# Two-head attention on one core: reciprocal three steps later, scaling one step later, SyncE's small transfers split and reordered

## The chip, the cores and the metric

One core of one Trainium2 chip runs the whole program. The metric is device microseconds of one execution. The kernel before took 3663.01 us (median of three; 3644.68 to 3670.26).

## The reference, cut to what matters

The program is a graph layer followed by a transformer block on x of shape (2, 2048, 512). Only the block's attention is touched by the change:

```
qkv = (h @ Wqkv + bqkv).reshape(B, L, 3, H, HD)        # B=2, L=2048, H=16, HD=32
attn = softmax(einsum('blhd,bmhd->bhlm', q, k) * HD ** -0.5, axis=-1)
out = einsum('bhlm,bmhd->blhd', attn, v).reshape(B, L, D)
return out @ Wproj + bproj
```

The softmax's division is done last: unnormalized exponentials are multiplied with the values, and the product is scaled by the reciprocal of the exponentials' sum.

## The kernel before, in words

The phases run one after the other: setup, graph layer, q/k/v projections, attention, output projection, MLP. Attention is `attention_phase`, and it is one straight program for each of the five engines; semaphores tie them together. Nothing schedules it at run time: the order on each engine is the order of the code.

The work is cut into 16 pairs g (two heads of one batch element). A pair has 32 steps. Steps 0 to 15 are its first half, steps 16 to 31 its second; a half is half of the query rows (1024 of 2048, for both heads), and a step is one tile of 128 keys against those rows, in four chunks c of 512 rows. Halves are numbered n = 0 to 31.

- **TensorE** (PE) makes per chunk one score matmul (`att_pS`, L1333) and one matmul for the row maxima of the next pair (`att_pM`, L1286). Score banks rotate over three, maxima banks over four, so TensorE waits for ScalarE or VectorE when one of them falls behind. At chunk 2 of each even step it also makes the value products of two earlier steps (`att_pO`, L1301). At step 4 of a half, chunk 2, it sums up the exponentials of the previous half (`finish`, L1315): 16 matmuls with a tile of ones (L1307).
- **ScalarE** (ACT) takes the exponential of each score chunk (L1218). At step 0, chunk 2, it copies the finished products of the half before to `oc` (L1190, function `copy`); before that it waits until the stores of the half before that one have left `oc` (`o_stored`, L1189). At step 4, chunk 2, it copies the sums to `rec` (L1198). It also issues the loads of a later pair (`LOADS`: steps 3, 6, 9, 12, 15, 18 and the values at step 2): six of these seven lie in a pair's first half.
- **VectorE** (DVE) reduces each maxima chunk (L1233). After the four chunks of step `INVERT` of a half it makes the reciprocal of the packed sums (L1252, function `invert`); it waits there for four small transfers (`z_packed`).
- **GpSimd** (POOL) adds up nine of a half's sixteen probability tiles with eight additions (L1155), sends four others to DMA additions (L1135), and, after addition number `SCALED`, scales the output of the half before: `oc` times `rec` (L1125, function `scale`), for which it waits for `z_spread`.
- **SyncE** (SP) issues the small transfers, in one order. For each half: the first two 1 MB copies of the DMA sums (`send_first`, L1077), then `reciprocals`: pack the sums of four rows into 128 partitions (L1084, four transfers), wait for the reciprocal, keep it in DRAM (L1086), wait for that to land, spread it over the partitions (L1089, four transfers). After that `store` (L1062) waits for the scaling and issues the four output stores (L1068). In a pair's second half SyncE also sends the turned maxima of the next pair (`rows`, L1055) between `reciprocals` and `store`.

The chain of a half's output is therefore: sums copied (L1198), packed, inverted on VectorE, kept, spread, scaled on GpSimd, stored, and then ScalarE may overwrite `oc` at step 0 of the next half.

Of the kernel before, what the change touches and what calls it, by code (L numbers as in the profile page):

```python
# [78 lines left out]
def raw(ap):  # L79

    return ap.bitcast(F32)
# [844 lines left out]
def attention_phase(nc, io, keep):  # L926

    with ExitStack() as ctx:
        m = Mem(nc, ctx, "att")
        NG = B * H // 2  # L930
# [13 lines left out]
        NA = len(ADDED) - 1  # L944
        FINISH = 4
        LOADS = [3, 6, 9, 12, 15, 18]
        INVERT = 6
        SCALED = 5
        ident = keep["ident"]

        qs = [m.sb(f"qs{i}", [KD + 2, 2, S], F32R) for i in range(U)]
# [30 lines left out]
        def m_tile(g, step, c):  # L982

            ahead = 1 if step < ST - LEAD else 2
            return (g + ahead, (step + LEAD) % ST * 4 + c) if g + ahead < NG else None
# [35 lines left out]
        def exps(g, step):  # L1021
            return turns_of[g, step, 3] + 1

        def turn(g):
            return place[f"turned {g}"]
# [8 lines left out]
        def load_part(eng, g, i):  # L1034
            k, at = g % U, slice(g % 2 * S, (g % 2 + 1) * S)
            if i < 3:
                dst, src = qs[k][i * HD:(i + 1) * HD], q_v[(0, 0, 1)[i], g // 2, :, :, at]
            else:
                dst, src = ks[k][(i - 3) * HD:(i - 2) * HD], k_v[(0, 1, 0)[i - 3], g // 2, :, :, at]
            eng.dma_start(raw(dst), src).then_inc(loaded[k], 16)  # L1040

        def load_values(eng, g):
            hp = g // 2
            eng.dma_start(V[g % 2][:], v_v[:, g % 2, :, hp * 2 * HD:(hp + 1) * 2 * HD]).then_inc(v_loaded[g % 2], 16)

        @block.sync
        def _(sp):
            def load(g):
                for i in range(6):
                    load_part(sp, g, i)  # L1050

            def load_v(g):
                load_values(sp, g)

            def rows(g):  # L1055

                sp.wait_ge(m_read, turn(g) + 1)
                for h in range(2):
                    sp.dma_start(raw(qs[g % U][KD + h:KD + h + 1]).rearrange("a h (t n) -> a (h t) n", n=P),
                                 raw(nm[:, h, :])).then_inc(top_rows[g % U], 16)  # L1060

            def store(n):  # L1062

                g, half = divmod(n, 2)
                sp.wait_ge(o_ready, n + 1)
                for c in range(4):
                    dst = o_v[g // 2, c // 2, :, g % 2, (2 * half + c % 2) * 512:(2 * half + c % 2 + 1) * 512]
                    sp.dma_start(dst, oc[c * HD:(c + 1) * HD]).then_inc(o_stored, 16)  # L1068

            def send_first(n):  # L1070

                if n >= 1:
                    sp.wait_ge(s_done, turns_of[n - 1] + 1)
                for i in range(2):
                    step = n % 2 * MT + CHAINS[i][0]
                    sp.wait_ge(exp_done, exps(n // 2, step))
                    sp.dma_start(gathered[i][:], prob[step % PR][:]).then_inc(first_sent[i], 16)  # L1077

            def reciprocals(n):

                sp.wait_ge(exp_done, turns_of[n] + 1)
                for c in range(4):
                    row = rec[c * HD:c * HD + 1, :].rearrange("a (i x) -> a i x", x=16)
                    sp.dma_start(packed[c * HD:(c + 1) * HD, :], row).then_inc(z_packed, 16)  # L1084
                sp.wait_ge(inverted, n + 1)
                sp.dma_start(io["z_d"][n % 2].rearrange("c (i x) -> (c i) x", x=16), packed[:]).then_inc(z_kept, 16)  # L1086
                sp.wait_ge(z_kept, 16 * (n + 1))
                for c in range(4):
                    sp.dma_start(rec[c * HD:(c + 1) * HD, :], io["z_d"][n % 2, c:c + 1, :].to_broadcast([HD, 512])).then_inc(z_spread, 16)  # L1089

            load(0)
            load(1)
            load_v(0)
            load_v(1)
            load(2)
            rows(0)
            for g in range(NG):
                if g >= 1:
                    send_first(2 * g)
                    reciprocals(2 * g - 1)  # L1100
                    store(2 * g - 1)
                else:
                    send_first(0)
                send_first(2 * g + 1)
                reciprocals(2 * g)
                if g + 1 < NG:
                    rows(g + 1)
                store(2 * g)
            reciprocals(2 * NG - 1)
            store(2 * NG - 1)  # L1110
            sp.wait_ge(o_stored, 64 * 2 * NG)

        @block.gpsimd
        def _(pool):
# [12 lines left out]
            def send(n, i, j):  # L1127

                step = n % 2 * MT + CHAINS[i][j]
                pool.wait_ge(exp_done, exps(n // 2, step))  # L1130
                if j == 1:
                    pool.wait_ge(first_sent[i], (n + 1) * 16)
                else:
                    pool.wait_ge(sent[i], (n * 2 + 1) * 16)
                nc.gpsimd.dma_start(gathered[i][:], prob[step % PR][:], accum_op=ALU.add).then_inc(sent[i], 16)  # L1135

            for g in range(NG):
                for half in range(2):
                    n = g * 2 + half
                    for i in range(1, NA + 1):  # L1140
                        step = half * MT + ADDED[i]
                        pool.wait_ge(exp_done, exps(g, step))
                        new = prob[step % PR]
                        if i == SCALED + 1 and n >= 1:
                            pool.wait_ge(o_ready, n)
# [10 lines left out]
                        if ADDED[i] in SENT_BEHIND:  # L1156
                            send(n, *SENT_BEHIND[ADDED[i]])
                        if i == SCALED and n >= 1:
                            pool.wait_ge(added, n * NA + i)
# [67 lines left out]
        def _(dve):  # L1227
            def maxima(g, q):
                if q == 0 and g >= 1:
                    dve.wait_ge(top_ready, g)  # L1230
                at = place[g, q]
                dve.wait_ge(m_done, at + 1)
                nc.vector.tensor_reduce(mx[:, q // 4, q % 4:q % 4 + 1], bank(at)[:], AX.X, ALU.max).then_inc(m_read, 1)  # L1233
# [15 lines left out]
            def invert(n):  # L1249

                dve.wait_ge(z_packed, 64 * (n + 1))
                nc.vector.reciprocal(packed[:], packed[:]).then_inc(inverted, 1)  # L1252
# [10 lines left out]
            for g in range(NG):  # L1263
                for step in range(ST):
# [5 lines left out]
                    for c in range(4):  # L1270
                        if m_tile(g, step, c):
                            maxima(*m_tile(g, step, c))
                    if step % MT == INVERT and n >= 0:
                        invert(n)
# [492 lines left out]
def build(nc, io, upto=9):  # L1767

    for name, shape, dt in [("x1_d", (B * S, D), F32), ("gate_d", (2, B * S // 512, P, D), F32),
                            ("qk_d", (2, 2, D, B * S), F32), ("v_d", (B * S, D), F32),  # L1770
                            ("o_d", (D, B * S), F32), ("z_d", (2, 4, 512), F32), ("x2_d", (B * S, D), F32), ("h2_d", (D, B * S), F32)]:
        io[name] = nc.dram_tensor(name, shape, dt, kind="Internal").ap()
    with ExitStack() as ctx:
        m = Mem(nc, ctx, "keep")
        keep = {"cols": m.sb("cols", [P, NCOLS]), "ident": m.sb("ident", [P, P]),
                "modA": m.sb("modA", [P, 2, B * S // 512 * DC]), "modB": m.sb("modB", [P, 2, B * S // 512 * DC])}
        with ExitStack() as early:
            e = Mem(nc, early, "graph")
            keep["floor4"] = e.sb("floor4", [4, 1])
            keep["wl_bc"] = e.sb("wl_bc", [P, 2 * NONGT * L])  # L1780
            keep["bb"] = e.sb("bb", [P, 1])
            keep["LW"] = e.sb("LW", [P, 2, B, DC, D + 2 * HM], F32R)
            keep["VB"] = e.sb("VB", [GM, B, 2, DC, P])
            keep["r4"] = e.sb("r4", [4, B, D + 2 * HM], F32R)
            setup_phase(nc, io, keep)
            graph_phase(nc, io, keep)
        if upto > 1:
            qkv_phase(nc, io, keep)
        if upto > 2:
            attention_phase(nc, io, keep)  # L1790
        if upto > 3:
            proj_phase(nc, io, keep)
        if upto > 4:
            mlp_phase(nc, io, keep)
# [45 lines left out]
```

## Time and profile before

| | |
|---|---|
| profiled execution | 3662.34 us |
| its span, first to last instruction | 3660.6 us |
| mean granted TensorE clock | 0.939 of full |
| TensorE matmul busy | 3351.8 us (92%) |
| VectorE busy | 2061.6 us (56%) |
| ScalarE busy | 1520.4 us (42%) |
| GpSimd busy | 1617.7 us (44%) |
| VectorE idle before the maxima reductions (L1233) | 366.1 us, for TensorE |
| TensorE idle before the maxima matmuls (L1286) | 115.6 us, 94.2 of it for VectorE |
| TensorE idle before the score matmuls (L1333) | 8.2 us, 7.9 of it for ScalarE |
| TensorE, 980 to 2650 us (attention without its end) | 1569.96 us busy of 1670.00, clock 0.96 |

The span is what lies between the first and the last instruction on the core; 1.7 us of the execution's time lie around it. A row of the timeline merges neighbouring instructions of one kind: its start, the time it covers, the count, and in brackets how long the engine stood idle before it and what ended that. Matmuls overlap, so the sum of their durations is more than the time they take. The clock is a share of 2.4 GHz, 0.5 being 1.2 GHz.

### The profile page before, as it was taken

How to read it: one execution, taken by the hardware profiler on the slowest of the kernel's cores; microseconds unless marked ns; L12 is line 12 of the kernel's file. 1: busy time of each engine (PE TensorE's matmuls, PEld its weight loads, DVE VectorE, ACT ScalarE, POOL GpSimd, SP SyncE). 2: the span in 40 equal slices, each digit the busy share in tenths (PEclk: the TensorE clock that was granted, in tenths of full speed). 3: DMA queues.
4: the chain of work that ended last, by engine and by line, in shares of the span. 5: the costliest groups of instructions: out<-in, count | busy, mean ns of one | idle time of the engine just before them, and what ended most of it. 6: DMA issues, size and time to landing. Idle time of an engine off the chain costs nothing. (4 is left out here: it accounts for less than half of the span.)

```text
span 3660.6 us, 45573 instructions
## 1 busy us (share of the span) xinstructions
PE 3351.8 (92%) x17004; PEld 2242.4 (61%) x17004; DVE 2061.6 (56%) x3419; ACT 1520.4 (42%) x2751; POOL 1617.7 (44%) x621
## 2 busy tenths in 40 slices
PE   7989996997999999999999999999995679999999
PEld 6478884775554544555545545445434568888887
DVE  1278884443976766767767767777506922221222
ACT  0011113432066655656656656566661242222222
POOL 1033331001087777777778767778884400000000
PEclk9899997998599999999999999999997889999999
DMA  4222324445256676676766666766564641111110
GB/s 151 81 83 89 98 79 158 171 155 174 64 133 161 145 167 149 147 167 149 169 156 159 155 163 149 169 153 150 128 150 165 231 153 46 41 41 37 37 32 24
DMA packets 202646, 460.45 MB, mean 126 GB/s; under 512 B 62811, under 2 KB 84571, under 8 KB 171742
## 3 DMA queue, kind: packets, MB, share of 16 engines
q1 hardware_dynamic: 144286, 267.16, 21.8%
q0 software_dynamic: 18432, 134.23, 18.5%
q10 hardware_dynamic: 39744, 56.63, 6.2%
q8 instruction: 113, 1.85, 0.2%
q14 instruction: 71, 0.58, 0.1%
HBM read 167.28 MB, written 88.34 MB: 70 GB/s over the span
## 5 line engine op out<-in xcount | busy, mean ns | idle before, releaser
L1233 DVE TENSOR_REDUCE att_mx<-att_pM 128x1 f32<-128x512 f32 x2048 | 1250.8, 681 | 366.1 <-PE att_pM L1286 365.4
L1218 ACT ACTIVATE att_prob<-att_pS 128x512 f32<-128x512 f32 x2048 | 1047.3, 618 | 576.6 <-PE att_pS L1333 574.6
L1155 POOL TENSOR_TENSOR att_acc<-att_acc,att_prob 128x2048 f32<-128x2048 f32 x224 | 1026.6, 4583 | 337.8 <-ACT att_prob L1218 323.7
L1286 PE MATMUL att_pM<-att_ks,att_qs 96*128 96x512 f32 x2048 | 863.2, 436 | 115.6 <-DVE att_mx L1233 94.2
L1333 PE MATMUL att_pS<-att_qs,att_ks 98*128 98x512 f32 x2048 | 855.0, 421 | 8.2 <-ACT att_prob L1218 7.9
L1333 PEld LDWEIGHTS att_pS<-att_qs,att_ks 98*128 98x128 f32 x2048 | 390.3, 191 | 358.0 <-issue 204.7
L1286 PEld LDWEIGHTS att_pM<-att_ks,att_qs 96*128 96x128 f32 x2048 | 412.0, 201 | 245.4 <-DVE att_mx L1233 167.7
L1301 PE MATMUL att_pO<-att_prob,att_V 128*32 128x512 f32 x4096 | 513.6, 621 | 0.0
L1696 DVE TENSOR_TENSOR mlp_us<-mlp_tu,mlp_us 128x512 fp32r<-128x512 f32 x128 | 89.6, 700 | 537.5 <-ACT mlp_us L1669 537.5
L1739 PE MATMUL mlp_pu<-mlp_hs,mlp_W 128*128 128x512 f32 x1536 | 371.3, 391 | 20.2 <-DVE mlp_W L1688 20.2
L1758 PE MATMUL mlp_pa<-mlp_W,mlp_us 128*128 128x512 f32 x1536 | 368.8, 389 | 0.0
L1739 PEld LDWEIGHTS mlp_pu<-mlp_hs,mlp_W 128*128 128x128 f32 x1536 | 290.0, 189 | 81.1 <-issue 20.6
L1758 PEld LDWEIGHTS mlp_pa<-mlp_W,mlp_us 128*128 128x128 f32 x1536 | 288.3, 188 | 59.8
L1681 POOL TENSOR_TENSOR mlp_hs<-mlp_hf,mlp_hs 128x512 fp32r<-128x512 f32 x32 | 41.3, 1291 | 600.5 <-ACT mlp_hs L1647 600.5
L1668 ACT ACTIVATE mlp_tu<-mlp_pu,keep_cols 128x512 f32<-128x512 f32 x128 | 88.3, 690 | 505.6 <-PE mlp_pu L1739 505.6
L1301 PEld LDWEIGHTS att_pO<-att_prob,att_V 128*32 128x32 f32 x4096 | 109.8, 112 | 259.9 <-ACT att_prob L1218 161.6
L1155 POOL TENSOR_TENSOR att_acc<-att_prob 128x2048 f32<-128x2048 f32 x32 | 146.8, 4589 | 190.2 <-ACT att_prob L1218 190.2
L921 PE MATMUL qkv_pq<-qkv_hs,qkv_W 128*128 128x512 f32 x768 | 188.8, 402 | 2.4 <-DVE qkv_hs L861 2.4
L921 PEld LDWEIGHTS qkv_pq<-qkv_hs,qkv_W 128*128 128x128 f32 x768 | 146.0, 193 | 32.9 <-issue 2.8
L1530 PE MATMUL prj_pp<-prj_W,prj_os 128*128 128x512 f32 x384 | 98.0, 419 | 47.6 <-POOL prj_os L1479 47.4
L1252 DVE RECIPROCAL att_packed<-att_packed 128x16 f32<-128x16 f32 x32 | 8.1, 253 | 230.3 <-DMA att_packed<-att_rec 230.3
L1115 POOL MEMSET att_ones<- 128x32 f32 x1 | 0.1, 125 | 306.8 <-POOLq L107 306.8
(183 smaller groups left out, 3042.5 us busy)
## 6 DMA issues: line engine op xcount, KB each, us to landing
att_gathered<-att_prob POOLq DMA_DIRECT2D x128, 1024.0 KB, 8.2
att_gathered<-att_prob SPq DMA_DIRECT2D x64, 1024.0 KB, 5.0
qk_d<-qkv_qs SPq DMA_DIRECT2D x64, 512.0 KB, 2.7
att_qs<-qk_d ACTq DMA_DIRECT2D x39, 512.0 KB, 4.7
att_ks<-qk_d ACTq DMA_DIRECT2D x39, 512.0 KB, 6.1
gat_xT<-in_xT SPq DMA_DIRECT2D x32, 256.0 KB, 3.2
gat_xrow<-in_x SPq DMA_DIRECT2D x32, 256.0 KB, 2.8
x_d<-gat_x SPq DMA_DIRECT2D x32, 256.0 KB, 2.1
```

What stands on the lines that cost most here:

```text
L921: last = nc.tensor.matmul(out[:], a, r, start=n + c == 0, stop=n == 2 and c == DC - 1)
L1155: nc.gpsimd.tensor_tensor(acc[half][:], old[:], new[:], ALU.add).then_inc(added, 1)
L1218: nc.scalar.activation(prob[step % PR][:, c, :], pS[at % 3][:], ACT.Exp, scale=SCALE).then_inc(exp_done, 1)
L1233: nc.vector.tensor_reduce(mx[:, q // 4, q % 4:q % 4 + 1], bank(at)[:], AX.X, ALU.max).then_inc(m_read, 1)
L1286: nc.tensor.matmul(bank(at)[:], qs[k][0:KD, h, t * P:(t + 1) * P], ks[k][0:KD, h, mc * 512:(mc + 1) * 512], start=True, stop=True).then_in ...
L1301: last = nc.tensor.matmul(pO[c * HD:(c + 1) * HD, :], V[g % 2][:, mt, (c // 2) * HD:(c // 2 + 1) * HD], prob[step % PR][:, c, :], start=mt ...
L1333: nc.tensor.matmul(pS[at % 3][:], ks[k][:, h, mt * P:(mt + 1) * P], qs[k][:, h, lc * 512:(lc + 1) * 512], start=True, stop=True).then_inc( ...
L1530: last = nc.tensor.matmul(pp[nt][:], os_[s][:, k, c, nt * P:(nt + 1) * P], W[:, w, c, :], start=n + c == 0, stop=n == 2 and c == DC - 1)
L1668: nc.scalar.activation(tu[j % 2][:], pu[j % 4][:], ACT.Gelu, bias=bias)
L1696: nc.vector.tensor_tensor(us[j % 2][:, 1, :], tu[j % 2][:], us[j % 2][:, 0, :], ALU.subtract).then_inc(u_lo, 1)
L1739: last = nc.tensor.matmul(pu[j % 4][:], W1[:, k, c, j * P:(j + 1) * P], hs[s][:, w, c, :], start=q + c == 0, stop=q == 2 and c == DC - 1)
L1758: last = nc.tensor.matmul(pa[nt][:], us[j % 2][:, k, nt * P:(nt + 1) * P], W2[:, w, j, :], start=j + q == 0, stop=j == MC - 1 and q == 2)
```

## The change

`INVERT` goes from 6 to 9: VectorE makes the reciprocal after the maxima of step 9 of a half. `SCALED` goes from 5 to 6: GpSimd scales after its sixth addition. `reciprocals` is cut in three functions, called one after the other everywhere but in a pair's second half, where the turned maxima now go out between the kept reciprocal and its spreading. No instruction is added or removed.

```diff
-        INVERT = 6
-        SCALED = 5
+        INVERT = 9
+        SCALED = 6
...
-            def reciprocals(n):
+            def pack(n):
...
+            def keep_inverted(n):
+
                 sp.wait_ge(inverted, n + 1)
                 sp.dma_start(io["z_d"][n % 2].rearrange("c (i x) -> (c i) x", x=16), packed[:]).then_inc(z_kept, 16)
+
+            def spread(n):
+
                 sp.wait_ge(z_kept, 16 * (n + 1))
...
                 send_first(2 * g + 1)
-                reciprocals(2 * g)
+                pack(2 * g)
+                keep_inverted(2 * g)
                 if g + 1 < NG:
                     rows(g + 1)
+                spread(2 * g)
                 store(2 * g)
```

The rows below are the order of instructions on an engine, with tile names and counts; line numbers of the kernel after are 12 higher from the split on (L1252 is L1264 there, L1125 is L1137).

VectorE before, one pair from a reciprocal in its second half to the next pair's (`att_mx` are the maxima, `att_top` and `att_nm` their final forms, `att_packed` the sums):

```order
L1252 RECIPROCAL att_packed<-att_packed 128x16
L1233 TENSOR_REDUCE att_mx<-att_pM 128x1 x12
L1237 TENSOR_REDUCE att_top<-att_mx 128x32
L1233 TENSOR_REDUCE att_mx<-att_pM 128x1 x4
L1245 CAST att_nm<-att_pM 32x128
L1247 TENSOR_TENSOR att_nm<-att_pM,att_nm 32x128
L1233 TENSOR_REDUCE att_mx<-att_pM 128x1 x48
```

VectorE in the changed kernel, the same place:

```order
L1264 RECIPROCAL att_packed<-att_packed 128x16
L1249 TENSOR_REDUCE att_top<-att_mx 128x32
L1245 TENSOR_REDUCE att_mx<-att_pM 128x1 x4
L1257 CAST att_nm<-att_pM 32x128
L1259 TENSOR_TENSOR att_nm<-att_pM,att_nm 32x128
L1245 TENSOR_REDUCE att_mx<-att_pM 128x1 x60
```

The reciprocal stands twelve reductions later, directly ahead of the pair's final maxima.

GpSimd before, from a half's fourth addition on (`att_oc` is the output being scaled):

```order
L1155 TENSOR_TENSOR att_acc<-att_acc,att_prob 128x2048
L1135 DMA att_gathered<-att_prob 128x2048
L1155 TENSOR_TENSOR att_acc<-att_acc,att_prob 128x2048
L1135 DMA att_gathered<-att_prob 128x2048
L1125 TENSOR_TENSOR att_oc<-att_oc,att_rec 128x512
L1155 TENSOR_TENSOR att_acc<-att_acc,att_prob 128x2048 x3
```

GpSimd in the changed kernel, the same place:

```order
L1167 TENSOR_TENSOR att_acc<-att_acc,att_prob 128x2048
L1147 DMA att_gathered<-att_prob 128x2048
L1167 TENSOR_TENSOR att_acc<-att_acc,att_prob 128x2048
L1147 DMA att_gathered<-att_prob 128x2048
L1167 TENSOR_TENSOR att_acc<-att_acc,att_prob 128x2048
L1137 TENSOR_TENSOR att_oc<-att_oc,att_rec 128x512
L1167 TENSOR_TENSOR att_acc<-att_acc,att_prob 128x2048 x2
```

The scaling stands behind one more addition, that of step 12.

SyncE before, in a pair's second half (`z_d` is the kept reciprocal, `att_nm` the turned maxima, `o_d` the output in DRAM):

```order
L1084 DMA att_packed<-att_rec 32x1x16 x4
L1086 DMA z_d<-att_packed 128x16
L1089 DMA att_rec<-z_d 32x512 x4
L1059 DMA att_qs<-att_nm 1x32x128 x2
L1068 DMA o_d<-att_oc 32x512 x4
```

SyncE in the changed kernel, the same place:

```order
L1084 DMA att_packed<-att_rec 32x1x16 x4
L1089 DMA z_d<-att_packed 128x16
L1059 DMA att_qs<-att_nm 1x32x128 x2
L1095 DMA att_rec<-z_d 32x512 x4
L1068 DMA o_d<-att_oc 32x512 x4
```

The spreading stands behind the two transfers of the turned maxima; in a pair's first half SyncE's order is as before.

## Rows read from the trace of the kernel before

**Rows 1.** Waits, 900 to 2650 us: who, for whom: us, times, longest.

```profile
DVE att_packed L1252 <- DMA att_packed<-att_rec: 109.9, 29, 7.4
PE att_pM L1286 <- DVE att_mx L1233: 94.2, 27, 6.8
...
ACT att_oc L1190 <- DMA o_d<-att_oc: 13.0, 5, 3.3
```

**Rows 2.** ScalarE timeline: start, busy us, work, count, idle before, releaser.

```profile
1059.43 0.60 ACT L1198 ACTIVATE att_rec<-att_pS 128x512 f32<-128x512 f32 x1 [4.75 <-PE att_pS L1307]
...
1382.17 0.60 ACT L1190 ACTIVATE att_oc<-att_pO 128x512 f32<-128x512 f32 x1 [3.25 <-DMA o_d<-att_oc]
...
1734.13 0.60 ACT L1198 ACTIVATE att_rec<-att_pS 128x512 f32<-128x512 f32 x1 [4.75 <-PE att_pS L1307]
...
1770.38 0.60 ACT L1190 ACTIVATE att_oc<-att_pO 128x512 f32<-128x512 f32 x1 [1.29 <-PE att_pO L1301]
...
1785.42 0.60 ACT L1198 ACTIVATE att_rec<-att_pS 128x512 f32<-128x512 f32 x1 [4.80 <-PE att_pS L1307]
...
1842.75 0.60 ACT L1198 ACTIVATE att_rec<-att_pS 128x512 f32<-128x512 f32 x1 [4.75 <-PE att_pS L1307]
...
2610.73 0.60 ACT L1198 ACTIVATE att_rec<-att_pS 128x512 f32<-128x512 f32 x1 [4.75 <-PE att_pS L1307]
```

**Rows 3.** VectorE's timeline, 1776 to 1798.1 us.

```profile
1776.84 4.88 DVE L1233 TENSOR_REDUCE att_mx<-att_pM 128x1 f32<-128x512 f32 x8 [0.94 <-PE att_pM L1286]
1786.06 4.88 DVE L1233 TENSOR_REDUCE att_mx<-att_pM 128x1 f32<-128x512 f32 x8 [4.35 <-PE att_pM L1286]
...
1797.95 0.25 DVE L1252 RECIPROCAL att_packed<-att_packed 128x16 f32<-128x16 f32 x1 [5.38 <-DMA att_packed<-att_rec]
```

**Rows 4.** TensorE's matmuls in its timeline, near 1383, 1799 and 1808 us.

```profile
1383.31 0.50 PE L1333 MATMUL att_pS<-att_qs,att_ks 98*128 98x512 f32 x1 [1.49 <-ACT att_prob L1218]
...
1798.81 0.80 PE L1286 MATMUL att_pM<-att_ks,att_qs 96*128 96x512 f32 x1 [4.86 <-DVE att_mx L1233]
...
1801.24 3.21 PE L1301 MATMUL att_pO<-att_prob,att_V 128*32 128x512 f32 x16
...
1808.32 1.92 PE L1301 MATMUL att_pO<-att_prob,att_V 128*32 128x512 f32 x16
```

**Rows 5.** SyncE timeline of DMA issues: start, us spent issuing, count.

```profile
1754.57 1.97 SPq L1059 DMA_DIRECT2D att_qs<-att_nm  x2
1760.55 4.21 SPq L1068 DMA_DIRECT2D o_d<-att_oc  x4
...
1798.23 0.35 SPq L1086 DMA_DIRECT2D z_d<-att_packed  x1
1805.84 2.87 SPq L1089 DMA_DIRECT2D att_rec<-z_d  x4
1818.14 4.12 SPq L1068 DMA_DIRECT2D o_d<-att_oc  x4
```

**Rows 6.** GpSimd's timeline, 1758 to 1775 us.

```profile
1758.97 1.55 POOL L1125 TENSOR_TENSOR att_oc<-att_oc,att_rec 128x512 f32<-128x512 f32 x1
1760.66 14.07 POOL L1155 TENSOR_TENSOR att_acc<-att_acc,att_prob 128x2048 f32<-128x2048 f32 x3
```

**Rows 7.** Stretches: length, busy us by engine, clock, DMA share, GB/s.

```profile
1766.13:1768.13 2.00, 2.00 (x11) 1.52 (x9) 2.00 (x4) 2.00 (x6) 2.00 (x1) 1.00 0.01 3
...
1810.13:1812.13 2.00, 2.00 (x12) 1.63 (x9) 1.18 (x2) 1.42 (x3) 1.59 (x3) 1.00 0.34 68
...
1826.13:1828.13 2.00, 2.00 (x18) 0.75 (x11) 1.30 (x3) 0.63 (x2) 1.86 (x2) 1.00 0.29 57
```

**Rows 8.** Landings of output stores (L1068), issued near 1760, 1818, 2758 us.

```profile
DMA to landing us min/median/max: 3.6/4.6/5.2
...
DMA to landing us min/median/max: 5.5/6.2/6.8
...
DMA to landing us min/median/max: 1.7/1.7/1.8
```

More of the change, by code:

```diff
@@ L1099, in _ @@
                     send_first(2 * g)
-                    reciprocals(2 * g - 1)
+                    pack(2 * g - 1)
+                    keep_inverted(2 * g - 1)
+                    spread(2 * g - 1)
                     store(2 * g - 1)
@@ L1104, in _ @@
                 send_first(2 * g + 1)
-                reciprocals(2 * g)
+                pack(2 * g)
+                keep_inverted(2 * g)
                 if g + 1 < NG:
                     rows(g + 1)
+                spread(2 * g)
                 store(2 * g)
-            reciprocals(2 * NG - 1)
+            pack(2 * NG - 1)
+            keep_inverted(2 * NG - 1)
+            spread(2 * NG - 1)
             store(2 * NG - 1)
```

## The prediction, made before the changed kernel had run

> **What bounds the kernel now.** I read the list of waits of the attention first, then the timelines of the five engines over two neighbouring halves, and last the DMA share of short stretches. The waits show TensorE as the engine that is almost always at work, and two places where it is made to stand. The reciprocal on VectorE waits 109.9 us in 29 times for the packed sums to land; behind it the maxima reductions are late, the four maxima banks fill, and TensorE stands 94.2 us in 27 times for a reduction [rows 1]. The other place is ScalarE's copy of the output, which waited 13.0 us in 5 times for the output stores before it [rows 1].
>
> Then I took the sums copy (L1198, once per half) as a clock of the loop. From the first to the copy of 2610.73 there are 28 periods, 1551.3 us [rows 2]. They alternate: the one from 1734.13 takes 51.3 us, the next, from 1785.42, takes 57.3 [rows 2]. Added up, the 14 short ones give 729.2 us and the 14 long ones 822.1. The long ones run mostly through a pair's first half, where four of the 0.5 MB loads are issued as well.
>
> What would a period be without a stop? VectorE's groups of eight reductions repeat every 0.94 + 4.88 = 5.82 us, and the group behind the sums comes 9.22 us after the one before it [rows 3]: 7 x 5.82 + 9.22 = 50.0 us. So 28 x 50.0 = 1400 us, and **151 us** are lost to stops: 29 in the short periods, 122 in the long ones.
>
> A stop costs more than its idle time. In the long period VectorE waited 5.38 us [rows 3], TensorE stood 4.86 us, and behind that 16 value matmuls took 3.21 us where they otherwise take 1.92 [rows 4]: TensorE ran at the lower of its two clock levels (1.2 for 2.4 GHz) for a few microseconds. The period is 57.3 - 50.0 = 7.3 us too long, so the slow stretch costs 7.3 - 4.9 = 2.4 us. Of the copy's wait, TensorE feels only a part: 3.25 us of waiting on ScalarE [rows 2] became 1.49 us on TensorE [rows 4], since it has score banks to work on; the cover is 1.76 us. That case too had slow matmuls behind it.
>
> **The change, part by part.** Times are counted from a period's sums copy.
>
> 1. *Reciprocal three steps later.* Three steps are 12 reductions, one and a half groups, 8.7 us. VectorE stood ready at 1797.95 - 5.38 = 1792.57 [rows 3], +7.15. It will be ready at +15.9. The sums landed at 1797.95, +12.5, in this long period; the longest of the 29 waits was 7.4 us [rows 1], which is +14.5. So all 29 waits are covered, with 1.4 us to spare in the worst. A load by ScalarE (step 9) that the stop used to delay now goes out at about +11 and may take a little of that; I keep small leftovers of 0.4 us a period. The reciprocal itself (0.25 us, rows 3) costs the same in either place, and TensorE's banks cover it. Removed: 151 us at most.
>
> 2. *Keeping and spreading.* SyncE now issues the kept reciprocal at about +16.2, where it was +12.8 in the long period [rows 5]. From there to the spreading it was 7.6 us [rows 5], the spreading takes 2.9 us to issue and the landing some 4: +30 to +33. In a short period the turned maxima are ready at 1754.57, +20.4 [rows 5], and their two issues (1.97 us) now stand ahead of the spreading. It goes out at about +21.3 to +22.5 instead of +12.9, and lands before +30. Who waits for it is GpSimd's scaling alone.
>
> 3. *Scaling one addition later.* It began at 1758.97 [rows 6], +24.8, and that period had 1.2 us of stop. An addition is 14.07 / 3 = 4.69 us [rows 6], and that of step 12 starts when that step's exponentials are there, 5.8 us after step 10's. I put the scaling 5.45 us later, at +29.1 without a stop, and its end 1.6 later at +30.7 [rows 6]. In the long period the spreading is not there yet: the scaling begins about +32 and ends at +33.6. GpSimd's two last additions move by the same few microseconds; they are needed only by the next sums, over 12 us later, so I cost that at nothing. The cover is gone if the scaling comes later than about +38.
>
> 4. *The output stores.* This is what is late next. `oc` must be empty when ScalarE reaches its copy: 1770.38, +36.25 [rows 2], less the 1.2 us of stop: +35.05. The four stores took 4.21 us to issue [rows 5] and the last up to 5.2 us to land in the short period, 4.12 [rows 5] and up to 6.8 in the long one; with nothing else under way, at the end of the attention, they landed in 1.7 [rows 8]. The quickest issue of four small transfers took 2.87 us [rows 5]. The bounds for the time from the scaling's end to an empty `oc` are thus 4.6 and 10.9 us. Which end holds is told by the DMA share. In the short period the DMA engines fall to 0.01 at 1766.13, +32.0 [rows 7]: the big transfers are out, and stores issued at about +30.8 land near the lower bound, around +35.4. No wait beyond the 1.76 us of cover. In the long period the DMA engines are at work until 1826.13 to 1828.13, +41 to +42, but with thin stretches behind the stop (0.34 at 1810.13, rows 7); with the stop gone the same work should be through at +38. Stores issued from +33.7 on then land about +39.5: ScalarE waits 4.5 us, TensorE stands 4.5 - 1.76 = 2.7 us, and 2.4 us of slow clock follow, 5.1 in all.
>
> In the last three halves there are no more maxima matmuls behind the reciprocal, so nothing is won there, and a late store may cost up to 5 us in all; I take 2.
>
> **The sum**, against the profiled execution's 3662.3 us (the median of the runs shown is 3663.0): the short periods win 29 and keep 14 x 0.4 = 6; the long ones win 122 and give back 14 x 5.1 = 71; the end costs 2. 3662.3 - 29 + 6 - 122 + 71 + 2 = **3590 us**.
>
> **What a page says of such transfers.** The row first: small transfers took 3.6 to 6.8 us to land while others were under way, and 1.7 when alone [rows 8]. The Trainium skill (DMA: Bandwidth & Descriptors, section Anatomy of one DMA) gives about 2.0 us of fixed cost for a DMA, mostly the receipt of the last write, and next to nothing more for 64 KB; it would put the landing of the small transfers at some 2 us in every period. By that rule the scaling would not wait, no copy would, and the sum would be that of rival A below. The rows of the crowded halves speak against it as a full account, the row at the end agrees with it.
>
> **The rivals.**
>
> *A. Everything is covered.* The DMA engines, with the stops gone, are through early enough that the stores of the long periods land within 35.05 + 1.76 = +36.8. That needs an end of the scaling by +32.2 with the lower bound of 4.6 us, and so a spreading landed by +30.6, the early edge of step 2. For it: in the long period the spreading took only 2.87 us to issue when the engines were thin. Against it: four loads and four 1 MB sums are in that half, and the spreading alone lands near +32. 3662 - 151 + 2 = 3513 us.
>
> *B. The stores of every period are late: slower.* `oc` becomes the bound. Where the stores take their crowded 9.4 us in the short periods too, `oc` is empty at +30.7 + 9.4 = +40.1, ScalarE waits 5.1, TensorE 3.3, with the slow clock 5.7 a period. In the long ones they take 10.9 behind a spreading of +33: empty at +45.5, a wait of 10.4, 8.7 + 2.4 = 11.1 a period. 14 x 5.7 + 14 x 11.1 = 235 given back for 151 won: 3662 + 84 + 2 = 3748 us. It decides from a landing of +37 in the short periods. For it: in the kernel before the copy was already late 5 times with the stores issued 5.5 us earlier. Against it: the 0.01 at +32.
>
> *C. An exchange.* The short periods are as forecast, but the long ones wait some 8.5 us for their stores (6.7 + 2.4 = 9.1 a period, 127 in all) because the DMA work is not compressed: 3662 - 29 + 6 - 122 + 127 + 2 = 3646 us, no difference.
>
> *D. The reciprocal still waits.* The sums land later than +15.9 because everything on the DMA engines moved up with them. Against it is the margin of 1.4 us over the worst of 29; a wait of 2 us in the long periods beside the forecast's would cost 14 x 4, some 3646 us again.
>
> **How the numbers follow.** Forecast 0.45, A 0.17, B 0.12, C 0.16, D 0.05, and 0.05 for something outside. The predicted time is 3590. The range reaches from past A, 3505, to past C and D, 3690; B's full price lies outside, and with the last 0.05 that is 0.17 left out. One per cent, about 37 us, is what a measurement of this kernel can tell from no change: its runs shown spread over 26 us. The forecast and A are faster by more than that; B is slower; C and D are within. So faster 0.66, within 1% 0.20, slower 0.14.
>
> **What the changed profile would show.** Step 1: VectorE's wait for the packed sums falls from 109.9 us to under 10, and with it TensorE's wait for the maxima. Steps 2 and 3: a new wait of GpSimd's scaling for the spread reciprocals, in the long periods only. Step 4: ScalarE's wait for the stores rises from 13 us to 50 to 70, in 14 periods, and TensorE's wait for the exponentials to some 40. The short periods should be 50 to 50.5 us, the long ones near 55. I am wrong if the short periods show the store wait too, if the long ones show none, or if the packed sums still hold VectorE.

## The result: 0.3% faster, an exchange of one wait for another

| | before | after |
|---|---|---|
| median us | 3656.4 | 3645.2 |
| ratio, 95% interval | | 0.9966 (0.9954 to 0.9979) |
| profiled execution's span | 3660.6 | 3638.3 |
| 28 periods of the loop | 1551.3 | 1530.1 |
| the 14 short, the 14 long | 729.2, 822.1 | 710.4, 819.7 |

The medians are over 20 runs each (3663.0 of the text above was that of three). 3590 us was forecast; the gain is 11 us, small but with 1 outside the ratio's interval, not 73. The list of waits of the changed kernel, 900 to 2650 us (who waits, for whom: us in total, times, longest):

```profile
ACT att_oc L1202 <- DMA o_d<-att_oc: 137.6, 27, 9.5
...
POOL att_oc L1137 <- DMA att_rec<-z_d: 131.2, 28, 9.2
PE att_pS L1345 <- ACT att_prob L1230: 93.3, 26, 7.9
...
DVE att_packed L1264 <- DMA att_packed<-att_rec: 39.8, 1, 39.8
```

VectorE's wait for the packed sums is gone from the loop: the one left, 39.8 us, is in the last pair, where VectorE has no maxima to reduce. TensorE's 94.2 us behind VectorE [rows 1] are gone too. In their place TensorE stands 93.3 us for exponentials, because ScalarE stands 137.6 us for the output stores, 13.0 before [rows 1]. The head of that chain is new as well: GpSimd's scaling waits 131.2 us for the spread reciprocals.

ScalarE's timeline (start, busy us, work, in brackets the idle time before it and its releaser): the first sums copy, one long period with its output copy, and the last sums copy of the 28 periods, answering to [rows 2].

```profile
1054.58 0.60 ACT L1210 ACTIVATE att_rec<-att_pS 128x512 f32<-128x512 f32 x1 [4.75 <-PE att_pS L1319]
...
1761.38 0.60 ACT L1210 ACTIVATE att_rec<-att_pS 128x512 f32<-128x512 f32 x1 [4.79 <-PE att_pS L1319]
...
1803.43 0.60 ACT L1202 ACTIVATE att_oc<-att_pO 128x512 f32<-128x512 f32 x1 [8.64 <-DMA o_d<-att_oc]
...
1822.08 0.60 ACT L1210 ACTIVATE att_rec<-att_pS 128x512 f32<-128x512 f32 x1 [4.75 <-PE att_pS L1319]
...
2584.68 0.60 ACT L1210 ACTIVATE att_rec<-att_pS 128x512 f32<-128x512 f32 x1 [4.75 <-PE att_pS L1319]
```

The long period takes 60.7 us, more than the 57.3 before. Now the same period engine by engine, with times from its start at 1761.38. VectorE's reciprocal, which has no idle time in front of it any more, where it had 5.38 [rows 3]:

```profile
1776.61 0.24 DVE L1264 RECIPROCAL att_packed<-att_packed 128x16 f32<-128x16 f32 x1
```

SyncE's issues (kept reciprocal, spreading, output stores), to be held against [rows 5]:

```profile
1776.88 0.35 SPq L1089 DMA_DIRECT2D z_d<-att_packed  x1
1788.53 2.35 SPq L1095 DMA_DIRECT2D att_rec<-z_d  x4
1800.30 1.73 SPq L1068 DMA_DIRECT2D o_d<-att_oc  x4
```

From the kept reciprocal (+15.5) to the spreading (+27.2) pass 11.7 us, where it was 7.6. What came into this stretch are GpSimd's third and fourth 1 MB additions by DMA, before:

```profile
1810.14 0.85 POOL L1135 DMA_DIRECT2D att_gathered<-att_prob  x1
...
1815.93 0.86 POOL L1135 DMA_DIRECT2D att_gathered<-att_prob  x1
```

and in the changed kernel:

```profile
1778.59 0.87 POOL L1147 DMA_DIRECT2D att_gathered<-att_prob  x1
...
1784.60 0.87 POOL L1147 DMA_DIRECT2D att_gathered<-att_prob  x1 [0.17 <-POOL att_acc L1167]
```

They moved from +24.7 and +30.5 to +17.2 and +23.2, and ScalarE's loads of steps 9 and 12 from +19.5 and +27.2 to +12.1 and +19.7. The DMA share of the stretch from +24 to +26 shows it, before and after (columns: length, busy us of PE, PEld, DVE, ACT, POOL, granted clock, DMA share, GB/s):

```profile
1809.42:1811.42 2.00, 2.00 (x13) 1.06 (x6) 1.08 (x3) 0.71 (x2) 1.59 (x3) 1.00 0.13 41
```

```profile
1785.38:1787.38 2.00, 2.00 (x11) 1.59 (x10) 2.00 (x4) 2.00 (x5) 1.83 (x2) 1.00 1.09 254
```

GpSimd's timeline shows the rest, against [rows 6]: the sixth addition, the scaling, two additions:

```profile
1785.64 4.58 POOL L1167 TENSOR_TENSOR att_acc<-att_acc,att_prob 128x2048 f32<-128x2048 f32 x1 [0.17 <-ACT att_prob L1230]
1799.01 1.26 POOL L1137 TENSOR_TENSOR att_oc<-att_oc,att_rec 128x512 f32<-128x512 f32 x1 [8.79 <-DMA att_rec<-z_d]
1800.40 9.19 POOL L1167 TENSOR_TENSOR att_acc<-att_acc,att_prob 128x2048 f32<-128x2048 f32 x2
```

The scaling begins at +37.6, 10.5 us after the spreading's first issue, after 8.79 us of waiting. The stores then go out in 1.73 us and have landed at 1803.43, +42.05, when ScalarE's copy starts. TensorE, against [rows 4], the first matmul after the stop and the value matmuls behind it:

```profile
1804.56 0.79 PE L1345 MATMUL att_pS<-att_qs,att_ks 98*128 98x512 f32 x1 [6.87 <-ACT att_prob L1230]
...
1809.13 3.64 PE L1313 MATMUL att_pO<-att_prob,att_V 128*32 128x512 f32 x16
```

It stood 6.87 us, and then 16 value matmuls took 3.64 us instead of 1.92: the lower clock level again (granted clock 0.50 from 1804 to 1812). Last, the stretches around the spreading's landing, against [rows 7]:

```profile
1789.38:1793.38 4.00, 4.00 (x26) 2.59 (x15) 3.07 (x6) 2.62 (x6) 0.84 (x1) 1.00 1.02 219
1793.38:1797.38 4.00, 4.00 (x26) 1.85 (x24) 3.09 (x6) 1.41 (x3) 0.00 (x0) 1.00 0.90 214
1797.38:1801.38 4.00, 0.31 (x2) 0.00 (x0) 1.29 (x3) 0.00 (x0) 2.24 (x2) 1.00 0.10 26
```

The DMA engines are full until about 1797, +36, and then fall to 0.10. In this period the spread reciprocals landed when the large transfers were out. The kept reciprocal had landed before that, by +27.1, with the engines still full; so it is not empty engines as such that a small transfer waits for (the run with the reciprocal two steps later shows more of this). Over all 14 long periods the spreading was issued at +24.8 on average, the scaling began at +36.8 and ScalarE's copy at +41.35.

The last of the 14 is a control within the same execution. It begins at 2534.86, and ScalarE issues no load in it, since no pair is left to load for:

```profile
2553.49 4.08 SPq L1095 DMA_DIRECT2D att_rec<-z_d  x4
...
2563.80 1.28 POOL L1137 TENSOR_TENSOR att_oc<-att_oc,att_rec 128x512 f32<-128x512 f32 x1
```

The spreading goes out at +18.6, the scaling begins at +28.9 without a wait, and the period takes 49.8 us.

### The profile page after: what moved, and what is told of

Same layout as the page of the kernel before. It is cut to its first block and busy times, and to the rows that moved or that the text cites. A ratio compares the mean times of both kernels' runs of the same rounds, so it can differ in the third digit from the quotient of the medians.

```text
span 3638.3 us, 45573 instructions
## 1 busy us (share of the span) xinstructions
PE 3336.3 (92%) x17004; PEld 2241.2 (62%) x17004; DVE 2061.6 (57%) x3419; ACT 1519.3 (42%) x2751; POOL 1615.4 (44%) x621
## 3 DMA queue, kind: packets, MB, share of 16 engines
q8 instruction: 113, 1.85, 0.2%
## 5 line engine op out<-in xcount | busy, mean ns | idle before, releaser
L1345 PE MATMUL att_pS<-att_qs,att_ks 98*128 98x512 f32 x2048 | 864.0, 425 | 96.1 <-ACT att_prob L1230 95.7
L1313 PE MATMUL att_pO<-att_prob,att_V 128*32 128x512 f32 x4096 | 503.5, 610 | 0.0
L576 ACT ACTIVATE gat_wT<-gat_p_wT 80x1024 f32<-80x1024 f32 x32 | 32.7, 1023 | 246.1 <-PE gat_p_wT L694 246.1
```

Of the source, the lines that this page charges most:

```text
L1313: last = nc.tensor.matmul(pO[c * HD:(c + 1) * HD, :], V[g % 2][:, mt, (c // 2) * HD:(c // 2 + 1) * HD], prob[step % PR][:, c, :], start=mt ...
L1345: nc.tensor.matmul(pS[at % 3][:], ks[k][:, h, mt * P:(mt + 1) * P], qs[k][:, h, lc * 512:(lc + 1) * 512], start=True, stop=True).then_inc( ...
```

## The experiments

Two theories stood first. **Theory 1**: crowding. In a pair's first half the 1 MB sums and the 0.5 MB loads fill the DMA engines, the small transfers of the reciprocal crawl, and the stores and ScalarE's copy come late. **Theory 2**: the new places of the scaling and of SyncE's transfers cost what the reciprocal's new place wins. A third, that two trips over DRAM are slow in themselves, was held against both. Each ratio is to the kernel before on the same chip, with its 95% interval.

### The reciprocal alone

```diff
-        INVERT = 6
+        INVERT = 9
```

> The kernel before with INVERT 9 and nothing else: the scaling stays behind the fifth addition, SyncE's order stays. Theory 1 (what came back is the wait for the spread reciprocals, which crawl while the DMA engines are full, then the stores, then ScalarE's copy): the long periods behave as in the changed kernel, since there the scaling waits for the spreading until about +37.5 wherever it stands; with three additions instead of two behind it, the next sums may come a little late. Long periods 59 to 60 us, short ones 50 to 51, 3640 to 3655 us. Theory 2 (the scaling's and SyncE's new places cost the time, and the reciprocal alone would win): long periods near 52, under 3580 us.

Measured: 3635.7 us, 0.9949 (0.9925 to 0.9973). Its waits:

```profile
POOL att_oc L1125 <- DMA att_rec<-z_d: 213.5, 29, 13.8
...
ACT att_oc L1190 <- DMA o_d<-att_oc: 107.1, 13, 9.4
PE att_pS L1333 <- ACT att_prob L1218: 86.0, 21, 7.7
```

Short periods 50.1 us on average, long ones 58.3, as theory 1 has it; the time is 4 us under its range. TensorE stands 86 us for exponentials with the scaling and SyncE's order untouched, so theory 2 falls: the exchange is a matter of the reciprocal's own lateness.

### The loads moved out of the crowd, in the changed kernel and in the one before

```diff
-        LOADS = [3, 6, 9, 12, 15, 18]
+        LOADS = [1, 2, 3, 17, 18, 19]
```

> The changed kernel with the six 0.5 MB loads of a pair issued at steps 1, 2, 3, 17, 18, 19 instead of 3, 6, 9, 12, 15, 18: in the stretches ahead of the sums, where the DMA engines are idle. Same transfers, same number. Theory 1 (crowding in a pair's first half): the spread reciprocals land before +30 in both halves, GpSimd's wait for them falls from 131 us to under 30, ScalarE's wait for the stores from 138 to under 30, the long periods become like the short ones (50.5 to 51.5), some 8 us each for 14 of them: 3645 - 110 = about 3530 us. Theory 3 (the two trips over DRAM are slow in themselves, whatever else is under way): the waits stay, 3635 to 3650 us.

Measured: 3523.4 us, 0.9633 (0.9609 to 0.9656). Its waits:

```profile
POOL att_oc L1137 <- DMA att_rec<-z_d: 36.9, 16, 11.5
...
ACT att_oc L1202 <- DMA o_d<-att_oc: 28.6, 14, 3.7
...
PE att_pS L1345 <- ACT att_prob L1230: 8.4, 21, 1.3
```

SyncE's issues in one of its formerly long periods, begun at 1714.29:

```profile
1729.81 0.35 SPq L1089 DMA_DIRECT2D z_d<-att_packed  x1
1734.88 3.09 SPq L1095 DMA_DIRECT2D att_rec<-z_d  x4
1744.57 1.74 SPq L1068 DMA_DIRECT2D o_d<-att_oc  x4
```

From keeping to spreading it is 5.1 us now, from the spreading to the scaling's start 8.4 at most, and the scaling begins at +29 with no wait. And the stretches of the DMA engines (columns as above):

```profile
1738.29:1742.29 4.00, 4.00 (x26) 2.53 (x28) 4.00 (x7) 3.70 (x8) 3.70 (x1) 1.00 1.11 250
1742.29:1746.29 4.00, 4.00 (x25) 2.61 (x18) 3.07 (x6) 2.58 (x6) 3.79 (x3) 1.00 0.49 107
1746.29:1750.29 4.00, 4.00 (x26) 1.88 (x25) 3.08 (x6) 2.69 (x7) 3.86 (x2) 1.00 0.12 33
```

The large transfers are out at about +30 instead of +36 (the DMA share is 0.66 from +29 to +30 and 0.00 from +30 to +31; what follows are the stores). All 14 long periods became 49.8 us, the time without a stop, and their sum fell from 819.7 to 697.7. The transfers are the same in number, size and route, so the third theory falls, and the 122 us that the long periods gave up are the price of crowding by the loads. Whether the small transfers queue in the DMA engines or at the memory behind them, no run separates. The short ones kept 710.1; in them lie 14 of the scaling's 16 waits, 23.8 us, and with the two behind the loop the total misses the forecast of under 30 us.

> The kernel before with the loads at steps 1, 2, 3, 17, 18, 19. Theory 1: the packed sums land at about +8 in every half, as they do in the short periods of the kernel before; the long periods lose their stop of some 5 us and the slow clock behind it, leaving 52 us or less each: 3656 - 14 x 7 = about 3560 us. Theory 3: packing is as slow as before, 3645 to 3660 us. Together with the run of the changed kernel with such loads it tells what the change is worth when the crowding is gone: 30 us by theory 1 (the short periods' stops).

Measured: 3571.7 us, 0.9771 (0.9748 to 0.9795), 12 us above the forecast. The waits of the kernel before with the moved loads:

```profile
DVE att_packed L1252 <- DMA att_packed<-att_rec: 134.0, 31, 50.2
...
PE att_pM L1286 <- DVE att_mx L1233: 30.4, 25, 3.3
```

The 134.0 us are mostly waits in the last pair. In the 28 periods the packed sums still hold VectorE, but for 0.6 to 3.9 us in the long ones instead of 5 to 7 (21.3 us in all, 88.1 with the old loads): long and short periods are alike (51.5 and 52.5). The change that brought 11 us with the old loads is worth 3571.7 - 3523.4 = 48 us with the moved ones; both ran on one chip.

### A dose of crowding

Of the four loads of the crowded stretch only the two early ones stay (first kernel) or only the two late ones (second):

```diff
-        LOADS = [3, 6, 9, 12, 15, 18]
+        LOADS = [1, 2, 3, 6, 9, 17]
```

```diff
-        LOADS = [3, 6, 9, 12, 15, 18]
+        LOADS = [1, 2, 3, 12, 15, 17]
```

> A dose: the changed kernel with loads at steps 1, 2, 3, 6, 9 and 17, so that two of the four 0.5 MB loads are left in the crowded stretch, the early ones (issued at about +2 and +11). Theory 1 in its form 'the small transfers land when the large ones issued up to then are out': both still delay the kept reciprocal, issued at +15.5, but the DMA work ends some 5 us earlier; the spreading lands about +32, the long periods take 51 to 53 us: 3535 to 3565 us. If the amount of crowding did not matter, only its presence, the long periods would stay near 59 and the time near 3640.

Measured: 3591.2 us, 0.9815 (0.9781 to 0.985).

```profile
ACT att_oc L1202 <- DMA o_d<-att_oc: 90.1, 28, 5.6
POOL att_oc L1137 <- DMA att_rec<-z_d: 87.0, 28, 5.4
```

> The other half of the dose: loads at steps 1, 2, 3, 12, 15 and 17; the two late ones are left (issued at about +20 and +29). Theory 1: the kept reciprocal lands as in a short period (spreading issued at about +19), so the spreading meets only the load of +20 and lands before +30; the load of +29 comes behind it. Long periods 50 to 51 us, 3525 to 3540 us, less than with the early loads. If only the total of the DMA work counts, the two halves of the dose give the same time.

Measured: 3575.8 us, 0.978 (0.9747 to 0.9814).

```profile
ACT att_oc L1202 <- DMA o_d<-att_oc: 86.0, 28, 5.1
...
POOL att_oc L1137 <- DMA att_rec<-z_d: 42.8, 28, 3.0
```

The excess of a long period over 49.8 us was 8.7 us with four loads, 4.8 with the two early ones, 4.7 with the two late ones (in the profiled executions), and 0.0 with none. Both runs lie above what was forecast, the second by a clear 35 us: the late loads hit another link of the chain. There the spreading goes out at +19.4 and the scaling begins at +29.9, as forecast, but the four stores are issued right behind the load of step 15, and in the period from 1854.37 they landed in:

```profile
DMA to landing us min/median/max: 4.3/4.7/5.2
```

With the early loads the stores of such a period land in 1.7 us, but the scaling begins only at +33.4. So large transfers ahead of the chain's end cost time whichever link they catch. That two early loads cost as much as two late ones holds for the profiled executions only, 3593.2 us for both kernels. That one is the slowest of the late kernel's five runs (the others 3573.8 to 3577.9), while the early kernel's four lie at 3585.5 to 3593.2: by the medians the late loads are 15 us cheaper, as was forecast, with intervals that overlap.

### ScalarE's copy one step later

```diff
-                        if step % MT == 0 and c == 2 and n >= 0:
+                        if step % MT == 1 and c == 2 and n >= 0:
                             copy(n)
```

> The changed kernel with ScalarE's copy of the output at step 1 instead of step 0, four exponentials (2.9 us) later; TensorE needs the bank only at step 2. Theory 1: every wait of ScalarE for the stores is 2.9 us shorter. In the short periods it vanishes; in the long ones about 8 us become 5, TensorE stands 2.9 us less in each of 14: 3645 - 14 x 2.9 - 5 = about 3600 us. Rival (ScalarE's wait is not what makes TensorE stand, or the copy's new place takes away cover): 3640 us or more.

Measured: 3616.3 us, 0.9892 (0.9867 to 0.9916), 16 us above the forecast; its waits:

```profile
PE att_pS L1345 <- ACT att_prob L1230: 64.3, 27, 6.2
ACT att_oc L1202 <- DMA o_d<-att_oc: 57.3, 13, 5.9
```

137.6 us of waiting for the stores became 57.3 and TensorE's 93.3 became 64.3. The long periods lost 2.15 us each (56.4) instead of 2.9. It shows that ScalarE's wait for the stores is a cause of TensorE's standing, and that the copy needn't be so early.

### The parts of the change taken back one at a time

```diff
-        SCALED = 6
+        SCALED = 5
```

> The changed kernel with SCALED back at 5. Theory 1: in the long periods the scaling waits for the spreading until about +37.5 anyway, so they stay at about 59 us; the short ones lose their 1.3 us of waiting for the stores and are 50 to 50.5; the last three halves are 5 us shorter. 3625 to 3640 us, against 3645 of the changed kernel. Rival (the later scaling is what wins): above 3650 us.

Measured: 3649.4 us, 0.9984 (0.9971 to 0.9997). Missed. GpSimd's wait:

```profile
POOL att_oc L1137 <- DMA att_rec<-z_d: 274.6, 29, 13.7
```

GpSimd now stands in front of its sixth addition for as long as the spreading takes, twice as long as before (131.2), and the end of the attention was not shorter (142.6 us for the last three halves, 140.0 in the changed kernel).

```diff
-                if g + 1 < NG:
-                    rows(g + 1)
                 spread(2 * g)
+                if g + 1 < NG:
+                    rows(g + 1)
                 store(2 * g)
```

> The changed kernel with SyncE's order as before: the spreading ahead of the turned maxima in a pair's second half. Theory 1: only short periods change; there the spreading goes out at about +19 instead of +21.3, the scaling begins at +29 instead of +31, no wait for the stores is left: 14 times 0.5 us, 3635 to 3645 us. Rival (the new order matters because it lets the turned maxima out in time): 3650 us or more.

Measured: 3636.2 us, 0.9946 (0.9928 to 0.9964).

```profile
POOL att_oc L1137 <- DMA att_rec<-z_d: 106.8, 13, 9.4
```

The scaling waits 13 times now, not 28: the short periods are free of it (50.1 us). By the medians SyncE's new order costs some 7 us; the intervals of 0.9946 and 0.9966 overlap, and the traces give 0.6 us in each of 14 short periods. With it, the later scaling is worth a few us at most (0.9966 against 0.9984, intervals that overlap too); with the old order it is worth nothing that could be told (0.9946 against 0.9949 for the reciprocal alone).

### The reciprocal two steps later

```diff
-        INVERT = 6
+        INVERT = 8
```

> The kernel before with INVERT 8 and nothing else, beside the run with INVERT 9 and nothing else (3636 us, 0.995 of before). VectorE is ready at about +12.9 instead of +15.2, so the kept reciprocal goes out up to 2.4 us earlier, and in some long periods the packed sums (landing at +12.5 to +14.5) hold VectorE again for up to 1.6 us. Theory 1a (the spreading lands when the large transfers of the half are out, about +36, whenever it is issued): the scaling begins at +36 to +38 as with INVERT 9, long periods 58 to 60 us, 3630 to 3645 us. Theory 1b (each small transfer takes its 10 to 11 us from its own issue): all moves up by 2.4 us, 14 x 2.4 = 34 us less, some 3605 us.

Measured: 3626.8 us, 0.9929 (0.9912 to 0.9947), between the two. The reciprocal was 1.6 us earlier in the long periods on average than with INVERT 9 alone, the scaling 1.1 us. It did not move evenly: in four of the 14 the scaling began between +31.6 and +33.5, in nine between +36.7 and +38.4, and in the last, which has no loads, at +26.6.

The trace shows what goes with the two groups: the order of the spreading and GpSimd's fourth 1 MB addition. In the four, the spreading's first issue stands 1.7 to 2.5 us ahead of that addition, in the nine 0.4 us ahead at most, or behind it. One of the four, from 1433.94:

```profile
1456.19 2.86 SPq L1089 DMA_DIRECT2D att_rec<-z_d  x4
...
1458.28 0.84 POOL L1135 DMA_DIRECT2D att_gathered<-att_prob  x1
```

Here the scaling began at +31.6, while the DMA share was 0.8 to 1.2 in every us from +20 to +37. So small transfers do land while the engines are full; what they seem to wait for is the large ones issued ahead of them. That is a correlation and not shown as the cause: no run moved the addition alone. In the run with INVERT 9 alone the one lead above 1 us (1.2) went with +33.8, but in the changed kernel one of 1.3 us went with +38.7. The waits of the whole run:

```profile
POOL att_oc L1125 <- DMA att_rec<-z_d: 189.4, 29, 14.0
...
ACT att_oc L1190 <- DMA o_d<-att_oc: 87.4, 13, 9.0
```

### A version that beats both

```diff
-        LOADS = [3, 6, 9, 12, 15, 18]
-        INVERT = 6
+        LOADS = [1, 2, 3, 17, 18, 19]
+        INVERT = 8
```

> The kernel before with the loads in the quiet stretches (steps 1, 2, 3, 17, 18, 19) and the reciprocal two steps later (INVERT 8); scaling and SyncE's order as before. With those loads the packed sums landed by +10.5 at the latest; INVERT 8 makes VectorE ready at about +13. Theory 1: no stop is left in any of the 28 periods, which are 49.8 to 50.1 us, the scaling at about +24 to +26 has the spread reciprocals in time, and the last three halves, without the later scaling, are 7 us shorter than in the run of the changed kernel with such loads (3523 us): 3505 to 3510 us. Rival: the later scaling and SyncE's new order are needed to win that much, and it stays at 3525 us or above.

Measured: 3515.0 us, 0.9609 (0.9574 to 0.9643). The first and the last of its 28 periods' sums copies:

```profile
1059.46 0.60 ACT L1198 ACTIVATE att_rec<-att_pS 128x512 f32<-128x512 f32 x1 [4.75 <-PE att_pS L1307]
...
2459.48 0.60 ACT L1198 ACTIVATE att_rec<-att_pS 128x512 f32<-128x512 f32 x1 [4.75 <-PE att_pS L1307]
```

1400.0 us for 28 periods: no stop is left, and 50.0 us a period is what the matmuls take. It needs neither the later scaling nor SyncE's new order; it came 5 us above its forecast range because the last three halves took 143 us, not 135.

## Why the prediction was wrong, step by step

1. **The potential and step 1 were right.** 151 us were lost to stops; the version without stops takes the 28 x 50.0 us worked out from VectorE's rows (49.8 a long period, 50.2 a short one). All waits for the packed sums in the loop vanished, and VectorE came to the reciprocal at +15.2 (forecast +15.9).

2. **Step 2 failed, in the long periods.** "The spreading takes 2.9 us to issue and the landing some 4: +30 to +33" took over the row of 7.6 us and the short landing from the kernel before. But there the spreading had met DMA engines that the stop itself had thinned out (share 0.13 where it is 1.09 now). Without the stop, the loads of steps 9 and 12 and two 1 MB sums move up into that very stretch. The loads' part is shown by moving them; the sums' part is read from the trace and was not tested. Keeping to spreading took 9.3 us on average and the spreading to the scaling 12.0: the scaling began at +36.8, 4.8 us later than assumed. About 1 us of it is the keeping (spreading issued at +24.8, by the forecast's terms at +23.8), the rest is the landing: in the period from 1761.38 the four spread transfers took 6.0 to 8.5 us to land, where "some 4" was assumed. The working had the right number in hand, DMA work "through at +38" (measured +36), and used it for the stores only, not for the spreading.

3. **Step 3** was right about the order and missed a wait: in the short periods too the spreading, issued at +21.3 as forecast, held the scaling until +31.0 (forecast +29.1). The run with SyncE's old order shows that this is the price of the turned maxima ahead of it; it costs 0.6 us a period. The prediction had named store waits in the short periods as a sign of being wrong, and they came: 13 of 14 short periods show one, 26.4 us in all, though TensorE felt at most 1.15 us of any.

4. **Step 4**: the last link was priced too high, which hid part of the error. Once the DMA engines were empty, each store took 1.7 us to land and the four 1.7 us to issue, so that `oc` was empty some 3.2 us after the scaling's end: less than the lower bound of 4.6 us, and 2.6 us less than the 5.8 (from +33.7 to +39.5) of the forecast. `oc` was empty at +41.35 instead of +39.5. The cover was counted too large as well: 1.76 us was the difference between ScalarE's whole wait and TensorE's, but the 4.5 us forecast were counted from the moment of an undisturbed copy, which itself is preceded by 1.3 us of waiting for TensorE [rows 2]. So TensorE's stop is the lateness less some 0.5 us, not less 1.8. The 2.4 us of slow clock were right on average only: what a long period lost against 49.8 us beyond TensorE's stop was 2.0 to 4.1 us in the 13 that had a stop (2.7 on average), and 4.0 in the period shown above.

The sum again: a long period had been put at 50.0 + 5.1 and took 58.55: 3.4 x 14 = 48 us, nearly all of it TensorE's stop. Of the 48, 1.85 x 14 = 26 are the later `oc` and 1.3 x 14 = 18 the cover; most of the rest is that an undisturbed copy stands at +34.8 and not at +35.05. The short ones took 50.74 instead of 50.4 (5 us), the end 4 us more than before instead of 2. 3590 + 48 + 5 + 2 = 3645. The profiled execution, which the sum started from, took 3640.0: the part ahead of the first sums copy was 4.9 us shorter in it (1054.58 against 1059.43). What happened looks like rival C, the exchange (3646 us, chance 0.16), in its effect: the long periods kept most of their length, the short ones won. C's reason did not hold. It had the stores late "because the DMA work is not compressed", but the large transfers were out at +36 instead of +41, the stores met empty engines, and it was the spreading that was caught. That C's 3646 comes so near is in part luck: it took the copy's lateness too large (8.5 us, measured 7.05 on average in the 13) and the cover too large as well, and the two errors cancel. B did not come, since the short periods' stores met empty engines, as the 0.01 of [rows 7] had said; A is what the moved loads gave (3523 us against its 3513).

The Trainium skill (DMA: Bandwidth & Descriptors, section Anatomy of one DMA) gives its 2.0 us of fixed cost for DMAs that GpSimd issues; the prediction applied it to SyncE's. For the stores the trace agrees (a median of 1.7 to 1.8 us to land in both kinds of period), for the spreading it does not (6.0 to 8.5 us): the traces put the difference on what else is under way.

## What to carry to other kernels

When a stop is removed, everything behind it moves up, its DMA traffic too: price each later transfer with the traffic that the stop-free schedule will have around it, not with the row that the stop has thinned out. Here a chain of small transfers was held up by the large ones issued around it, and the cheapest cure was to issue those in the quiet stretch: one line of step numbers was worth 2.3% by itself and 3.7% (with the whole change) to 3.9% (with `INVERT` 8 alone) with a later reciprocal, against 0.3% for the change. And before a wait is moved, follow its chain to the last buffer that is reused: the copy of `oc` was already late five times in 30.

## What the runs showed of the hardware that was not expected

- Small SyncE transfers took much longer to land beside large ones. The 64 KB output stores landed in 1.7 us when nothing else was under way. In the long period from 1761.38, at a DMA share of 0.9 to 1.15, the 2 KB packing transfers took 7.4 to 9.2 us, the 8 KB kept reciprocal 11.6 and the 64 KB spreading transfers 6.0 to 8.5. Their issue slows as well: four output stores took 1.73 us to issue on empty engines, 4.1 on full ones.
- The lower clock level followed the long stops whatever their cause: behind 4.86 us of waiting for VectorE [rows 4] and behind 6.87 us of waiting for ScalarE. In these two periods it cost 2.6 and 4.0 us (against 49.8 us and beyond the stop). Short stops went either way in the kernel before: behind 1.49 us [rows 4] the granted clock fell to 0.50, behind 2.07 us at 1521.5 it stayed at 1.00.
